# Reading the distance tables of an attention kernel by 16 rows per transfer instead of 32

## What is computed

```
scores = einsum('bhqd,bhkd->bhqk', q, k) / scale
rel = build_relative_position(S, S, BUCKETS, MAX_REL)      # log buckets of q - k
c2p_att = einsum('bhqd,hpd->bhqp', q, pos_k)
c2p = take_along_axis(c2p_att, clip(rel + ATT_SPAN, 0, 2 * ATT_SPAN - 1), axis=-1)
p2c_att = einsum('bhkd,hpd->bhkp', k, pos_k)
p2c = swapaxes(take_along_axis(p2c_att, clip(-rel + ATT_SPAN, 0, 2 * ATT_SPAN - 1), axis=-1), -1, -2)
scores = scores + (c2p + p2c) / scale
probs = softmax(scores); ctx = einsum('bhqk,bhkd->bhqd', probs, v)
```

## Time and profile before

| | |
|---|---|
| runs | 2462.11, 2466.71, 2465.15 us; median 2465.15 |
| profiled execution | 2483.14 us, span 2481.5 us |
| mean granted TensorE clock | 0.885 |
| busy, share of the span | PE 75%, DVE 65%, ACT 40%, POOL 46% |
| SP's transfers (hardware queue) | 267484 packets, 392 MB, 49.2% of 16 engines |
| attention stage | about 165 to 1190 us |

### The profile page before, as it was taken

How to read it: one execution, slowest core, us unless ns; L and a number is a source line. 1 busy time by engine, 2 the same in 40 slices (tenths; PEclk the granted TensorE clock), 3 DMA queues, 4 the chain that set the end, 5 groups by cost and what they waited for, 6 DMA issues and landing times. The chain is left out here.

```text
span 2481.5 us, 47249 instructions
## 1 busy us (share of the span) xinstructions
PE 1868.5 (75%) x13556; PEld 1379.0 (56%) x13557; DVE 1613.3 (65%) x3925; ACT 999.9 (40%) x2052; POOL 1130.0 (46%) x1472
## 2 busy tenths in 40 slices
PE   5868887888888888888599997756243389999652
PEld 3436666766666676666366764433233168876321
DVE  8947777777768777777755551687765944443354
ACT  2436665656656666655123232432031033332000
POOL 4135555555555555553131210377640045554666
PEclk9979999999999999999799998877575589999876
DMA  4679999999999999999312200000010545547333
GB/s 156 212 251 334 324 335 331 317 324 309 343 313 339 323 337 328 336 329 287 108 50 68 68 0 3 0 0 1 0 51 17 203 124 154 155 146 125 104 107 114
DMA packets 296148, 460.84 MB, mean 186 GB/s; under 512 B 38316, under 2 KB 229532, under 8 KB 295964
## 3 DMA queue, kind: packets, MB, share of 16 engines
q1 hardware_dynamic: 267484, 392.06, 49.2%
q0 software_dynamic: 28480, 66.39, 10.4%
HBM read 236.91 MB, written 221.38 MB: 185 GB/s over the span
## 5 line engine op out<-in xcount | busy, mean ns | idle before, releaser
L986 DVE CUSTOM_DVE_ANT_0 c2p<-bank,c2p 128x512 f32<-128x512 f32 x512 | 351.2, 686 | 176.3 <-PE bank L882 161.8
L944 ACT ACTIVATE c2p<-c2p,neg_max 128x512 f32<-128x512 f32 x512 | 372.0, 727 | 14.9 <-DVE neg_max L986 14.9
L995 DVE COPY probsT<-bank 128x512 f32<-128x512 f32 x512 | 351.1, 686 | 5.2 <-PE bank L892 5.1
L959 ACT COPY a_stage<-bank 128x320 f32<-128x320 f32 (+1 forms) x512 | 211.4, 413 | 308.8 <-PE bank L851 234.5
L892 PE MATMUL bank<-ident,c2p 128*128 128x128 f32 x2048 | 316.4, 277 | 1.2 <-ACT c2p L944 0.9
L892 PEld LDWEIGHTS bank<-ident,c2p 128*128 128x128 f32 x2048 | 256.8, 144 | 10.2 <-issue 2.6
L2260 POOL DMA_INDIRECT p_x_tile<-y_d,p_token x160 | 152.9, 956 | 230.2 <-POOLq L1961 107.5
L863 PE MATMUL bank<-tab,k 96*128 96x320 bf16 (+1 forms) x512 | 159.0, 311 | 121.8 <-DVE b_stage L938 104.1
L882 PE MATMUL bank<-ident,p2c 128*128 128x128 f32 x1280 | 233.7, 282 | 0.0
L938 DVE COPY b_stage<-bank 128x288 f32<-128x288 f32 (+1 forms) x256 | 119.7, 468 | 103.3 <-issue 50.2
L877 PE MATMUL bank<-k,q 96*128 96x384 bf16 (+1 forms) x512 | 158.9, 310 | 31.7 <-issue 26.4
(11 more groups left out here) (295 smaller groups left out, 3959.9 us busy)
## 6 DMA issues: line engine op xcount, KB each, us to landing
p2c_d<-b_stage SPq DMA_DIRECT2D x64, 640.0 KB, 8.2
c2p_d<-a_stage SPq DMA_DIRECT2D x64, 640.0 KB, 5.8
p2c_d<-b_stage SPq DMA_DIRECT2D x64, 576.0 KB, 7.6
c2p_d<-a_stage SPq DMA_DIRECT2D x64, 576.0 KB, 6.0
p2c<-p2c_d SPq DMA_DIRECT2D x256, 144.0 KB, 4.6
c2p<-c2p_d SPq DMA_DIRECT2D x256, 144.0 KB, 5.1
o_sorted_d<-p_o_pair SPq DMA_DIRECT2D x80, 256.0 KB
p_w_all<-in_experts SPq DMA_DIRECT2D x4, 3072.0 KB, 21.9
```

Of the source, the lines that this page charges most:

```text
L944: act.activation(c2p[:, w % 4, j, :], c2p[:, w % 4, j, :], ACT.Exp, bias=neg_max[:, w % 2, j:j + 1], scale=-1.0).then_inc(exp_done, 1)
L959: act.copy(staged(a_stage, wa % 2, wa % TPB)[:, j, :], bank[A_BANK][:, 0:width(wa % TPB)]).then_inc(a_copied, 1)
L986: dve.tensor_tensor_reduce(c2p[:, w % 4, j, :], bank[S_BANKS[(HB * w + j) % 3]][:], c2p[:, w % 4, j, :], -SCALE, LOWEST, ALU.add, ALU.min, ...
L995: dve.tensor_copy(probsT[:, wp % 2, j], bank[T_BANKS[j % 2]][:].rearrange("p (k q) -> p k q", k=TPB)).then_inc(probsT_copied, 1)
```

## The change

ROWS becomes a pair, one value for each side, both 16. A table has 2 * 128 + 2 * 16 = 288 columns (t = 1 and 2) or 272 (t = 0 and 3). `read_skewed` issues 8 transfers per table, each of 16 rows with up to 272 columns, and the waits count 128 for a table. The ranges that are filled with a constant reach 16 columns further to the middle. The helpers take the side as a new argument; DRAM tensors, staging buffers, `tab6`, the stores at line 356 and the calls of the helpers follow. The cut diff:

```diff
@@ -21,8 +21,10 @@
-ROWS = 32
-FIRST_X, TABLE = P - ROWS, 2 * P + 2 * ROWS
+ROWS = (16, 16)
+FIRST_X, TABLE = [P - r for r in ROWS], [2 * P + 2 * r for r in ROWS]
...
@@ -539,7 +541,7 @@
-        a_stage = sb(early3, "a_stage", [P, 2, 4 * TABLE], side="right")
+        a_stage = sb(early3, "a_stage", [P, 2, 4 * max(TABLE[0], C)], side="right")
...
@@ -566,41 +568,41 @@
-        def varied(t, g):
+        def varied(side, t, g):
...
-            return max(lo, ROWS * g), min(hi, ROWS * g + 2 * P + ROWS)
-        def constant(t):
+            return max(lo, ROWS[side] * g), min(hi, ROWS[side] * g + 2 * P + ROWS[side])
+        def constant(side, t):
...
-            sides = []
-            if lo < P - ROWS:
-                sides.append((0, lo, P - ROWS))
-            if hi > 2 * P + ROWS:
-                sides.append((1, 2 * P + ROWS, hi))
-            return sides
+            ranges = []
+            if lo < P - ROWS[side]:
+                ranges.append((0, lo, P - ROWS[side]))
+            if hi > 2 * P + ROWS[side]:
+                ranges.append((1, 2 * P + ROWS[side], hi))
+            return ranges
...
-        def first_col(t):
-            return ROWS if t == 0 else 0
-        def width(t):
-            return TABLE - ROWS if t in (0, TPB - 1) else TABLE
-        def end_cols(t):
-            last = width(t) - 1
+        def first_col(side, t):
+            return ROWS[side] if t == 0 else 0
+        def width(side, t):
+            return TABLE[side] - ROWS[side] if t in (0, TPB - 1) else TABLE[side]
+        def end_cols(side, t):
+            last = width(side, t) - 1
...
-            return stage[:, u, 0:HB * width(t)].rearrange("p (b x) -> p b x", b=HB)
+            return stage[:, u, 0:HB * width(int(stage is b_stage), t)].rearrange("p (b x) -> p b x", b=HB)
...
@@ -671,26 +673,29 @@
+            C2P_READ, P2C_READ = [16 * (P // r) for r in ROWS]
...
-                    def written(table_d, w):
+                    def written(side, table_d, w):
...
-                        return table_d[w % (2 * TPB), 0:P * HB * width(t)].rearrange("(p b x) -> p b x", p=P, b=HB)
+                        return table_d[w % (2 * TPB), 0:P * HB * width(side, t)].rearrange("(p b x) -> p b x", p=P, b=HB)
...
-                    def read_skewed(table_d, slot, t, dest, left, done):
-                        for g in range(P // ROWS):
-                            j0, j1 = varied(t, g)
-                            start = slot * P * HB * TABLE + ROWS * g * HB * width(t) + ROWS - 1 - ROWS * g - first_col(t)
+                    def read_skewed(side, table_d, slot, t, dest, left, done):
+                        rows, its_width = ROWS[side], width(side, t)
+                        for g in range(P // rows):
+                            j0, j1 = varied(side, t, g)
+                            start = (slot * P * HB * TABLE[side] + rows * g * HB * its_width + rows - 1 - rows * g
+                                     - first_col(side, t))
...
-                                           [[HB * width(t) - 1, ROWS], [width(t), HB], [1, j1 - j0]])
-                            sp.dma_start(dest[g * ROWS:(g + 1) * ROWS, :, j0 + left:j1 + left], skew).then_inc(done, 16)
+                                           [[HB * its_width - 1, rows], [its_width, HB], [1, j1 - j0]])
+                            sp.dma_start(dest[g * rows:(g + 1) * rows, :, j0 + left:j1 + left], skew).then_inc(done, 16)
...
```

More of the change, by code:

```diff
@@ L105, in build @@
         far_stack_d = dram("far_stack_d", [H, FAR, B * S], BF16)
[L106 to L109, removed]
+        c2p_stack_d = dram("c2p_stack_d", [H, STACK, D, TABLE[0]], BF16)
+        p2c_stack_d = dram("p2c_stack_d", [H, STACK, D, TABLE[1]], BF16)
+        c2p_d = dram("c2p_d", [2 * TPB, P * (B // 2) * TABLE[0]], F32)
+        p2c_d = dram("p2c_d", [2 * TPB, P * (B // 2) * TABLE[1]], F32)
         v_d = dram("v_d", [H, P, TILES, D + 1], F32)
@@ L220, in load_head @@
             for side, stack_d in enumerate((c2p_stack_d, p2c_stack_d)):
-                eng.dma_start(tab6[:, par, side, :], stack_d[ds(h, 1)].rearrange("h k d n -> (h k d) n")).then_inc(done, 16)
+                eng.dma_start(tab6[:, par, side, 0:TABLE[side]], stack_d[ds(h, 1)].rearrange("h k d n -> (h k d) n")).then_inc(done, 16)
         with ExitStack() as st:
@@ L705, in step @@
                             sp.wait_ge(p2c_filled, BODY * i3 + w3 + 1)
-                            read_skewed(p2c_d, w3 % (2 * TPB), kt, p2c[:, w3 % (2 * TPB)], 0, p2c_loaded[kt])
+                            read_skewed(1, p2c_d, w3 % (2 * TPB), kt, p2c[:, w3 % (2 * TPB)], 0, p2c_loaded[kt])
                         if is_unit(i2, w2):
@@ L711, in step @@
                             sp.wait_ge(c2p_filled, BODY * i2 + w2 + 1)
-                            read_skewed(c2p_d, w2 % (2 * TPB), t, c2p[:, w2 % 4], (t - 1) * P, c2p_loaded[w2 % 4])
+                            read_skewed(0, c2p_d, w2 % (2 * TPB), t, c2p[:, w2 % 4], (t - 1) * P, c2p_loaded[w2 % 4])
                         if w % 8 == 2 and is_unit(i, w) and is_unit(*ahead(i, w, 6)):
@@ L720, in step @@
                             sp.wait_ge(a_copied, HB * (BODY * ia + wa) + HB)
-                            sp.dma_start(written(c2p_d, wa), staged(a_stage, wa % 2, wa % TPB)).then_inc(a_written[wa % 2], 16)
+                            sp.dma_start(written(0, c2p_d, wa), staged(a_stage, wa % 2, wa % TPB)).then_inc(a_written[wa % 2], 16)
                         if is_unit(ib, wb):
@@ L763, in step @@
                             apart(pool)
-                            for side, c0, c1 in constant(t):
+                            for side, c0, c1 in constant(1, t):
                                 last = fill(p2c[:, w3 % (2 * TPB)], end_p2c[:, t], side, c0, c1)
@@ L773, in step @@
                             apart(pool)
-                            for side, c0, c1 in constant(t):
+                            for side, c0, c1 in constant(0, t):
                                 last = fill(c2p[:, w2 % 4], end_c2p[:, w2 % 4], side,
@@ L793, in step, with copy_ends @@
                         ib, wb = ahead(i, w, B_LEAD)
-                        def copy_ends(w, stage, ends_of, copied):
+                        def copy_ends(table, w, stage, ends_of, copied):
                             t = w % TPB
@@ L798, in copy_ends @@
                             pool.tensor_copy(ends_of[:, w % 4, ends(t), :].rearrange("p s b -> p b s"),
-                                             staged(stage, w % 2, t)[:, :, end_cols(t)]).then_inc(copied, 1)
+                                             staged(stage, w % 2, t)[:, :, end_cols(table, t)]).then_inc(copied, 1)
                         if is_unit(ia, wa):
@@ L870, in scores @@
                             for kt in ((0, 1), (2,), (3,), ())[t]:
-                                pe.wait_ge(p2c_loaded[kt], 64 * (4 * i + g + 1))
+                                pe.wait_ge(p2c_loaded[kt], P2C_READ * (4 * i + g + 1))
                         s = HB * w + j
```

26 lines of the change are left out of this document (13 added, 13 removed).

## The result

| | before | changed |
|---|---|---|
| median of 4 runs | 2464.32 us | 2866.15 us |
| lowest to highest | 2462.11 to 2466.71 | 2857.93 to 2869.09 |
| ratio, 95% interval | | 1.163 (1.1605 to 1.1657) |
| span of the profiled execution | 2481.5 us | 2856.3 us |

The change costs 402 us. 165 were forecast, and the range ended at 2740. SP's issue is the new bound, as forecast, but it takes 10.9 us per unit and not 9.1.

The account below looks back on a forecast made before the run. It took DMA work to bound the kernel at 7.8 us per unit and SP's issue to bound the changed one at 9.1; (9.1 - 7.8) x 127 = 165 us on 2465 gave 2630 us, range 2550 to 2740.

Parts of the forecast that it names:

- What bounds the kernel before: Attention stage: the 16 DMA engines set the pace, 8.0 us per unit by the sum against 7.8 measured.
- One more issue costs 0.48 us with half the pieces: SP's table reads: each added read of 64 pieces costs 0.48 us of issue, 0.43 as the low end.
- Case C: SP's reads: issue pitch falls under 0.40 us and bytes decide; at 0.37, 55 us faster, 2410 us; chance 0.06.
- SP's issue becomes the bound and SP waits for nobody: Attention stage: 16 reads and 2 writes issued by SP take 9.1 us per unit, others wait; 165 us more.
- It also removes what holds SP back now, since the queues run empty between bursts: SP's read groups: surplus over 1.8 us per four reads, put down to full DMA queues, vanishes with fewer bytes.
- if all holding stayed: Upper bound for SP's step: read groups keep 0.6 us surplus, two per unit; 10.3 us, +318, 2783 us.
- The bytes: Table writes and reads: smaller tables cut DMA work to 7.5 us per unit, 0.43 less; DMA share about 0.85.
- Case B: Table reads into 16 partitions run slower, perhaps at 118 GB/s: 11.6 us per unit, +483, 2950 us; chance 0.12.
- The lower clock: TensorE: at a granted clock of 0.85 its 6.6 us per unit become 7.5, still under 9.1; no own case.
- The range: Whole kernel: from 2550 us, just above the low issue pitch's time, past half of the holding (2706) to 2740.

Follow-up runs that it names:

- e12: Kernel before (32 rows), its table writes from the ninth unit on storing only the first of four sequences: 2361 us, ratio 0.961.
- e10: Kernel before with 64 rows per read transfer on both sides, so 4 reads a unit: 2530 us, ratio 1.028.
- e11: Kernel before (32 rows) with both table writes of a unit issued by ScalarE instead of SP: 2507 us, ratio 1.022.
- e1: Kernel before (32 rows, its bytes) with each read cut in two by sequences, so 16 reads a unit: 2917 us, ratio 1.173.
- e6: Changed kernel with the eight c2p reads of a unit issued by ScalarE instead of SP: 2738 us, ratio 1.097.
- e9: Changed kernel, its table writes from the ninth unit on storing only the first of four sequences: 2740 us, ratio 1.114.
- e8: Changed kernel with 16 rows on the c2p side alone (p2c 32) and both table writes issued by ScalarE: 2598 us, ratio 1.040.
- e4: Changed kernel with the eight reads of a table issued in row-group order 0, 1, 4, 5, 2, 3, 6, 7: 2898 us, ratio 1.163.
- e7: Changed kernel with both table writes of a unit issued by ScalarE instead of SP: 2789 us, ratio 1.117.
- e5: Changed kernel with SP's write of the c2p table moved between the p2c reads and the c2p reads: 2858 us, ratio 1.144.

## Why the prediction was wrong, point by point

- **What bounds the kernel before: right.** Less DMA time wins (e12: 1.6 us of it a unit, 0.8 won), more of it costs (e10), and fewer issues on SP win nothing (e10, e11).
- **One more issue costs 0.48 us with half the pieces: right.** Medians of 426 and 428 ns with 64 pieces, 0.47 of pitch. Undisturbed groups of eight take 3.61 to 3.64 us, 3.72 were forecast. It is the same from 16 to 128 pieces, but not at 256 (e10). Case C (a cheap issue) did not come about.
- **SP's issue becomes the bound and SP waits for nobody: right.** 3.5 us of waits in 200, VectorE waiting for c2p tables, short landings of the writes. e1 adds issues alone and e6 moves issues alone, and the time follows them.
- **"It also removes what holds SP back now, since the queues run empty between bursts": wrong, and this is the step that failed.** It rested on putting the surplus of the groups in rows 5 "down to the full DMA queues". The queues did run emptier (share 0.80, landing of a write 3.8 instead of 8.2 us) and the surplus stayed: 4.43 instead of 3.72 us for a mean group of eight, 1.4 us per unit. In the kernel before a mean group of four between 300 and 1100 us takes 2.46 us instead of 1.8, 1.3 us per unit: the holding was carried over whole. The larger part of it goes with the bytes that were written just before (e9), which the change reduces by 8% only; the DMA engines need not be full for it. Another 0.4 stand in the rest of SP's step, its writes, the ctx store and the loads of v, 0.2 of it waits of SP, most of them for GpSimd's fills. 9.1 + 1.4 + 0.4 = 10.9. In (10.9 - 9.1) x 127 that is 229 us, which with the forecast 165 makes 394 of the 402. Even the bound "if all holding stayed", 10.3, was too low. The six groups that it was read from are not the reason, since all groups between 300 and 1100 us would have made it 10.4; what it lacked are the 0.4 us outside the groups.
- **The bytes: wrong.** The DMA work was to fall to 7.5 us a unit and the share to 0.85. It is 0.80 x 10.9 = 8.7 us, more than the 1.04 x 7.8 = 8.1 of before. e1, with the bytes of before, has 0.77 x 11.1 = 8.6. Summed over the packets between 300 and 1100 us, the writes of tables did follow the bytes (2.9 instead of 3.1 us of the 16 engines a unit); the reads of tables did not (4.3 instead of 3.9 us). They have as many pieces as before, about 1015 a unit, and a piece took 68 instead of 61 ns although it is shorter. Why is open. It changed nothing for the change itself, but e8 met it.
- **Case B (narrow transfers):** its 2950 us came nearer than the forecast, but e1, e4 and e6 speak against its mechanism.
- **The lower clock hurts nobody: right,** see below.
- **The range** took in only half of the holding. With the cause of a stall not shown, its whole size belonged into the range. That would have carried it to about 2790 us, still short of 2866, mostly by what SP's step takes outside the reads.

What the rows don't settle: of the 1.8 us a unit over the forecast, the 0.9 that go with the written bytes are shown (e9), and that the holding reaches SP from another queue's writes (e7); the mechanism in between is not. The other 0.9 us were not tested. A hint stands in the trace of e9: of its 77 issues over 0.65 us between 300 and 1100 us, 71% had a packet of over 1 KB of the profile's queue q8 (instruction) start during them or in the 1 us before, of the shorter issues 2%. No run changed that, so it stays a hint.

The Trainium skill, "DMA: Bandwidth & Descriptors", section "Issuing engines are not separate DMA queues", says that the time to start a DMA on a sequencer is usually small relative to the DMA. This kernel is the case in which it is not: a 68 KB read costs 0.47 us of SP, 16 of them 7.5 us of a unit of 10.9. The same section holds that issuing on several engines saves only that time; here that time was worth 1.2 us a unit (e6).

## What to carry to other kernels

An issuing queue has a bound of its own: count the transfers per step, times 0.47 us on SP here (0.6 at 256 pieces), and compare with the step's time before cutting transfers smaller to save bytes. 6% fewer bytes of tables for twice the reads cost 16%. When a queue's issues show long ones among short ones, find out what they go with (here the bytes written just before, from whichever queue) before forecasting that they vanish; until then the whole stall stands in the range.

## What was not expected of the hardware

**TensorE's clock fell where TensorE waited.** The prediction had reckoned with 0.85. The clock was granted at 0.96 to 0.97 in rows 2 and at 0.83 in the changed kernel. A stretch, in the columns of before:

```profile
606.00:612.00 6.00, 1.46 (x14) 0.97 (x18) 2.47 (x7) 2.05 (x5) 3.62 (x5) 0.89 0.79 262
612.00:616.00 4.00, 4.00 (x44) 3.18 (x37) 1.50 (x4) 1.24 (x3) 0.00 (x0) 0.50 0.57 117
```

In 6 us PE worked for 1.46; in the 4 us after, the clock was 0.50, that is 1.2 GHz of its two levels of 1.2 and 2.4, and PE was busy throughout. The transposes of the probabilities take 307 ns in the mean instead of 277:

```profile
L897 PE MATMUL bank<-ident,c2p 128*128 128x128 f32 x2048 | 362.3, 307 | 6.2 <-ACT c2p L949 6.0
```

It cost next to nothing here, since SP waited only 4 of 800 us for copies; a kernel in which TensorE is next to the bound could not take that for granted.

**A write of a table holds a later issue by its bytes, across queues.** One write of 544 or 576 KB makes the second issue behind it some 0.4 us longer when it stands alone (e5, 825 instead of 426 ns in the median), with a quarter of its bytes nothing (e9, 424 ns, behind two writes).
